# Attention and expert feed-forward on one core: the second split moved into the next feed-forward, attention shifted by 16 units, a ring of 13, division by the softmax sums in token rows, one dense projection

## What is computed

```python
# attention, 8 heads of 16 channels, over all 768 tokens of a batch
xf = layernorm(x)
q, k, v = xf @ Wq, xf @ Wk, xf @ Wv              # split into heads
att = q @ k.T / sqrt(16) + bias_time + bias_part # bias_part by pair of particles
att = where(causal in time, att, -inf)           # k's time step <= q's
x = x + (softmax(att) @ v).reshape(B, L, C) @ Wo

# feed-forward: 8 experts' weights, both top-2 gate values applied to all of them
p1, p2 = normalised top-2 of softmax(layernorm(x) @ Wg)
for p in (p1, p2):
    h = gelu((layernorm(x) * p) @ W1[e] + b1[e]) # for every expert e, width 512
    out += sum over e of h @ W2[e] + b2_sum
x = x + out
```

## Time and profile before

| | before |
| --- | --- |
| median of 3 runs | 2374.73 us (2370.79 to 2376.21) |
| the profiled execution's own time | 2375.36 us |
| its span, first to last instruction | 2373.6 us |
| PE busy | 93% |
| PEld busy | 85% |
| ACT busy | 68% |
| DVE busy | 55% |
| POOL busy | 45% |
| mean granted clock of TensorE | 0.969 |

### The profile page before, as it was taken

One profiled execution on the slowest core, in us unless ns is written; L12 is line 12 of the kernel. 1 busy time (PEld: TensorE's weight loads), 2 busy tenths in 40 slices (PEclk: granted clock), 3 DMA queues, 4 the chain that ended last, 5 costly groups with the idle time before them and its releaser, 6 DMA issues.

```text
span 2373.6 us, 48113 instructions
## 1 busy us (share of the span) xinstructions
PE 2212.2 (93%) x18213; PEld 2028.0 (85%) x18213; DVE 1309.2 (55%) x3191; ACT 1615.2 (68%) x2730; POOL 1063.1 (45%) x1051
## 2 busy tenths in 40 slices
PE   3779999999999999999998999999999999999998
PEld 2569898898988889898997988889898898988898
DVE  6246454755546466454755546466454755546453
ACT  2447677576776757677576776857677576776876
POOL 5124344443445344344443444344344443444366
PEclk7789999999999999999999999999999999999999
DMA  3412030220402212030220402212030220402200
GB/s 47 92 31 38 8 46 13 36 30 11 51 9 32 30 29 38 8 48 12 36 30 11 52 11 30 30 29 37 8 48 12 36 30 11 52 11 30 30 5 8
DMA packets 68528, 68.68 MB, mean 29 GB/s; under 512 B 20286, under 2 KB 53962, under 8 KB 68298
## 3 DMA queue, kind: packets, MB, share of 16 engines
q1 hardware_dynamic: 67634, 65.34, 19.4%
q10 hardware_dynamic: 664, 0.27, 0.0%
HBM read 10.83 MB, written 6.29 MB: 7 GB/s over the span
## 4 chain that ended last, share of the span: by engine, by line
PE 67%; DVE 17%; ACT 9%; issue 5%; POOL 1%; SPq 1%; DMA 0%; ACTq 0%; DVEq 0%; POOLq 0%
PE acc L925 20%; DVE maxes L682 7%; PE zps L914 6%; PE wide L857 6%; ACT z L535 6%; PE zps L916 6%; PE zps L915 6%; PE wide L845 5%; PE wide L828 4%; DVE h L745 3%; PE wide L871 2%; PE wide L879 2%; PE wide L864 2%; PE acc L902 2%; PE wide L811 1%
## 5 line engine op out<-in xcount | busy, mean ns | idle before, releaser
L469 POOL TENSOR_TENSOR h<-h 128x384 f32<-128x384 f32 x1024 | 1022.3, 1008 | 1236.3 <-ACT h L561 1225.6
L560 ACT ACTIVATE h<-zps,b_col 128x384 f32<-128x384 f32 x1024 | 591.6, 578 | 405.6 <-DVE h L745 346.7
L745 DVE TENSOR_TENSOR h<-zps,ratio_b 128x384 f32<-128x384 f32 x1024 | 542.3, 552 | 539.7 <-PE zps L916 528.5
L925 PE MATMUL acc<-w,h 128*128 128x128 f32 x6144 | 821.2, 277 | 0.2 <-DVE outt L754 0.2
L925 PEld LDWEIGHTS acc<-w,h 128*128 128x128 f32 x6144 | 800.5, 193 | 3.8 <-issue 0.5
L561 ACT ACTIVATE h<-h,b_col 128x384 f32<-128x384 f32 x1024 | 621.4, 607 | 0.0
L682 DVE TENSOR_REDUCE maxes<-wide 128x1 f32<-128x128 f32 (+5 forms) x768 | 430.2, 615 | 295.1 <-PE wide L828 293.6
L914 PE MATMUL zps<-x_hi,w_lo 128*128 128x384 f32 x1024 | 388.6, 379 | 11.5 <-ACT h L560 10.2
L535 ACT ACTIVATE z<-wide 128x896 f32<-128x896 f32 (+2 forms) x384 | 335.1, 916 | 33.9 <-PE wide L845 25.9
L915 PE MATMUL zps<-x_lo,w_hi 128*128 128x384 f32 x1024 | 347.9, 340 | 0.0
L916 PE MATMUL zps<-x_hi,w_hi 128*128 128x384 f32 x1024 | 347.1, 339 | 0.0
(11 more groups left out here) (99 smaller groups left out, 1469.3 us busy)
## 6 DMA issues: line engine op xcount, KB each, us to landing
stack<-halves SPq DMA_DIRECT2D x384, 96.0 KB, 3.1
stack<-halves SPq DMA_DIRECT2D x384, 24.0 KB, 2.6
out_dram<-outt SPq DMA_DIRECT2D x256, 24.0 KB, 1.6
x_in<-in_x SPq DMA_DIRECT2D x124, 48.0 KB, 2.4
stack<-max_rows SPq DMA_DIRECT2D x128, 3.0 KB
stack<-max_rows SPq DMA_DIRECT2D x128, 1.5 KB
w<-in_L_ffn_W SPq DMA_DIRECT2D x8, 256.0 KB, 4.0
stack<-z SPq DMA_DIRECT2D x2, 180.0 KB
```

The costliest lines, as they stand in the source:

```text
L469: pool.tensor_tensor(h1[:, PLACE[m], :], h0[:, m % 2, :], h1[:, PLACE[m], :], ALU.add).then_inc(hsum_ready, 1)
L560: act.activation(h0[:, m % 2, :], zps[BANK[m]][:, 0:CT], ACT.Gelu, bias=b1_col[:, j:j + 1]).then_inc(h0_ready, 1)
L745: vec.tensor_tensor(h1[:, PLACE[m], :], zps[BANK[m]][:, 0:CT], ratio_b[:, c * CT:(c + 1) * CT], ALU.mult).then_inc(z1_ready, 1)
L925: ins = pe.matmul(acc[:, n * P:(n + 1) * P], h1[:, PLACE[k], n * P:(n + 1) * P], w2[:, j, :], start=(j == 0 and n == 0), stop=(j == UNITS_ ...
```

## The change

Split 1 of a batch moves from slot 60 of the feed-forward before to slot 15.5 of the batch's own feed-forward; its second half of `xn` gets a buffer of its own (`xn_last`). All other attention steps come earlier, in most cases by some 6 to 16 slots, so that the first ones of a batch lie up to 16.5 slots before the feed-forward of the batch before begins. The ring has 13 places. The three runs of filler matmuls are gone. `sums` and `divide` are replaced: `tokens` transposes the mixed values with their sums into token rows, VectorE divides there, and `back` transposes 2 x 3 tiles back; the projection is one matmul per tile with a dense Wo. The output is added into `res` instead of `outt`. Round 0 has its own order (`squeezed`, `FIRSTS_ALONE`), and so has the last (`FIRSTS_LAST`).

```diff
-LAG = 4
-RING = 10
-FIRSTS = (2, 2, 1, 0, 1, 3, 0, 1, 2, 1, 2, 0, 2, 0, 2, 1, 0, 1, 1, 2, 0, 0, 0, 0, 0, 0, 0, 2, 3, 3, 0, 0,
-          1, 2, 1, 2, 2, 1, 0, 1, 3, 1, 0, 0, 0, 0, 2, 2, 3, 0, 1, 3, 1, 0, 0, 1, 0, 1, 0, 0, 0, 2, 0, 2)
-AT = {("stats", 0): -6.5, ("seed", 0): -5.0, ("root", 0): -5.0, ("scale", 0): -3.5, ("turn", 0): 0, ("query", 0): 0.5,
-      ("key", 0): 1.0, ("value", 0): 2.0, ("rows", 0): 16.5, ("mix", 0): 28.0, ("sums", 0): 32.5, ("divide", 0): 34.0,
-      ("rows", 1): 40.0, ("mix", 1): 46.5, ("sums", 1): 48.0, ("divide", 1): 51.0, ("project", 0): 52.0, ("project", 1): 52.0,
-      ("stats", 1): 52.0, ("turn", 1): 54.5, ("seed", 1): 54.5, ("root", 1): 56.0, ("gate", 0): 57.0, ("weigh", 0): 60.0,
-      ("split", 0): 60.0, ("split", 1): 60.0}
+LAG = 5
+FIRST_LAG = 5
+KNOTS = ((-4.950000000000001, 3.0), (10.5, 10.5))
...
+RESIDUAL_AT = 15
+RING = 13
+FIRSTS = (2, 1, 1, 2, 2, 0, 1, 3, 1, 0, 2, 2, 0, 1, 2, 1, 0, 0, 0, 0, 0, 1, 2, 3, 1, 1, 1, 1, 1, 3, 1, 3,
+          0, 0, 0, 0, 0, 0, 2, 2, 3, 3, 1, 1, 0, 2, 0, 1, 1, 0, 0, 0, 0, 0, 0, 0, 0, 2, 0, 2, 1, 2, 1, 1)
+AT = {("stats", 0): -16.5, ("seed", 0): -12.5, ("root", 0): -10.0, ("scale", 0): -7.0, ("turn", 0): -6.5, ("query", 0): -4.0,
+      ("key", 0): -4.0, ("value", 0): -1.5, ("rows", 0): 13.5, ("split", 1): 15.5, ("mix", 0): 23.0, ("rows", 1): 31.0,
+      ("tokens", 0): 31.0, ("mix", 1): 38.5, ("tokens", 1): 40.0, ("back", 0): 41.0, ("back", 1): 41.0, ("project", 0): 41.5,
+      ("project", 1): 42.0, ("stats", 1): 43.0, ("turn", 1): 43.0, ("seed", 1): 43.5, ("root", 1): 45.0, ("gate", 0): 47.0,
+      ("weigh", 0): 54.0, ("split", 0): 54.5}
+MAXIMA_AT = ((1.0, 1.5, 2.5, 3.5, 4.0, 5.0, 7.0, 7.5, 7.5, 10.0, 11.0, 12.0),
+             (22.0, 22.0, 22.5, 23.0, 23.5, 23.5, 24.5, 26.5, 28.0, 29.0, 30.0, 30.5))
+SCORES_AT = ((17.0, 17.5, 18.5, 18.5, 19.0, 19.0, 19.0, 20.0, 20.0, 20.0, 20.5, 21.0),
+             (32.5, 34.5, 34.5, 35.0, 35.5, 35.5, 36.0, 37.0, 37.0, 37.0, 37.5, 38.0))
...
+            for m in range(FIRST_LAG):
                 unit(first, m)
...
-                    if r.b > 0 and a == 0:
-                        vec.wait_ge(out_ready, r.at(CHUNKS, 1 - CHUNKS + 1))
...
+                if r.b > 0:
+                    vec.wait_ge(out_stored, r.at(16 * TPT * CHUNKS, 16 * (TPT * (c + 1 - CHUNKS) + 1)))
...
-                    if hh == 0 and part == 0:
-                        idle(w[:, 0:P], 3)
...
-                    if hh == 0 and part == 1:
-                        idle(acc[:, CT:CT + P], 5, start=False)
...
+                elif step == "tokens":
                     pe.wait_ge(*taken(r, "mix", a))
                     for i in range(TILES):
-                        ins = pe.matmul(w[:, i * GH:(i + 1) * GH], mixed[:, i * P:(i + 1) * P], pick[:, :], start=True, stop=True)
+                        ins = pe.transpose(w[:, i * P:(i + 1) * P], mixed[:, i * P:(i + 1) * P], ident[:, :])
                     ins.then_inc(wide_filled[s], 1)
...
+                elif step == "back":
+                    pe.wait_ge(*taken(r, "tokens", 1))
+                    for n in range(HT):
+                        ins = pe.transpose(w[:, n * P:(n + 1) * P], share[:, a * HT + n, :], ident[:, :])
                     ins.then_inc(wide_filled[s], 1)
                 elif step == "project":
-                    pe.wait_ge(*taken(r, "divide", 1))
+                    pe.wait_ge(*taken(r, "back", a))
                     for n in range(HT):
                         i = a * HT + n
-                        for g in range(GROUPS):
-                            ins = pe.matmul(w[:, n * P:(n + 1) * P], mixed_n[g][:, i * P:(i + 1) * P], wo_pad[:, g, :],
-                                            start=(g == 0), stop=(g == GROUPS - 1))
+                        ins = pe.matmul(w[:, n * P:(n + 1) * P], act_t[:, i * P:(i + 1) * P], wo[:, :], start=True, stop=True)
                     ins.then_inc(wide_filled[s], 1)
...
                 elif step == "split":
-                    if a == 0:
-                        idle(w[:, 0:P], 8)
-                    pe.wait_ge(xn_ready, r.at(4, 3 + a))
+                    pe.wait_ge(weighed, Round(r.b - a).at(2, 1 + a))
```

More of the change, by code:

```diff
@@ L76, in attention_plan @@
     plan += [(AT["mix", g], "mix", g) for g in range(GROUPS)]
-    plan += [(AT[step, g], step, g) for g in range(GROUPS) for step in ("sums", "divide")]
+    plan += [(AT[step, n], step, n) for step in ("tokens", "back") for n in range(2)]
     plan += parts("maxima", 1, MAXIMA_AT[1]) + [(AT["rows", 1], "rows", 1)] + parts("scores", 1, SCORES_AT[1])
@@ L87 @@
 PLAN = attention_plan()
-WIDE_STEPS = ("turn", "query", "key", "value", "maxima", "rows", "scores", "mix", "sums", "divide", "project", "gate", "split")
+WIDE_STEPS = ("turn", "query", "key", "value", "maxima", "rows", "scores", "mix", "tokens", "back", "project", "gate", "split")
 WIDE = {(s, a): n for n, (s, a) in enumerate([(s, a) for _, s, a in PLAN if s in WIDE_STEPS])}
@@ L96 @@
 assert sum(FIRSTS) == UNITS
+assert sum(FIRSTS_ALONE) + FIRST_LAG == UNITS + LAG and sum(FIRSTS_LAST) + LAG == UNITS
 def places(count):
@@ L114, with squeezed @@
 BANK_BACK = back(BANK)
+def squeezed(slot):
+    x0, y0 = PLAN[0][0], 0.0
+    for x, y in KNOTS:
+        if slot < x:
+            return int(2 * (y0 + (slot - x0) * (y - y0) / (x - x0))) / 2
+        x0, y0 = x, y
+    return slot
 class Round:
@@ L262, in build, with rounds, run @@
         block = ctx.enter_context(nc.Block())
-        def rounds(eng, attention, unit, after, prepare=None):
+        def rounds(eng, attention, unit, after, prepare=None, skipped=None):
             first = Round(0)
+            def run(r, step, a):
+                due = r.b > 0 if (step, a) == ("split", 1) else r.b < BATCHES
+                if due:
+                    attention(r, step, a)
+                elif skipped and (step, a) in WIDE and WIDE[step, a] <= WIDE["split", 1]:
+                    skipped(r, step, a)
             for _, step, a in PLAN:
-                attention(first, step, a)
+                run(first, step, a)
                 if prepare:
                     prepare(first, step, a)
[L276 to L279, removed]
+            for m in range(FIRST_LAG):
                 unit(first, m)
@@ L284, in steps @@
                     for r, start in ((following, 0), (ahead, UNITS)):
[L285 to L289, removed]
+                        for slot, step, a in PLAN:
+                            at = squeezed(slot) if r.b == 1 else slot + start
+                            if lo <= at < hi and r.b <= BATCHES:
+                                run(r, step, a)
+                m, firsts = LAG, FIRSTS
+                if this.b == 0:
+                    m, firsts = FIRST_LAG, FIRSTS_ALONE
+                elif this.b + 1 == BATCHES:
+                    firsts = FIRSTS_LAST
                 for k in range(UNITS):
                     steps(k, k + 0.5)
-                    for _ in range(FIRSTS[k]):
+                    for _ in range(firsts[k]):
                         if m < UNITS:
                             unit(this, m)
-                        elif following:
+                        elif following.b < BATCHES:
                             unit(following, m - UNITS)
@@ L897, in attention, with skipped @@
                     ins.then_inc(wide_filled[s], 1)
-            def idle(to, count, start=True):
-                for _ in range(count):
-                    pe.matmul(to, ident[:, :], ident[:, :], start=start, stop=start, skip_group_check=not start)
+            def skipped(r, step, a):
+                s, free, _ = wide_at(r, step, a)
+                if free > 0:
+                    pe.wait_ge(wide_free[s], free)
+                pe.sem_inc(wide_filled[s], 1)
+                pe.sem_inc(wide_free[s], 1)
             def unit(r, m):
@@ L927, in after @@
                 ins.then_inc(hsum_used, 1)
[L929 removed]
+            rounds(pe, attention, unit, after, prepare=prepare, skipped=skipped)
 WEIGHT_DMAS = 4
[L933 to L934 removed]
+POOL_SMALL = 11
+POOL_SET = 14
 BIAS_LOADS = 6
```

114 lines of the change are left out of this document (58 added, 56 removed).

## The result

The changed kernel took 2216.93 us, the median of 4 runs (2216.19 to 2218.14); the kernel before took 2375.47 (2370.79 to 2377.47) beside it. The ratio is 0.9336 with a 95% interval of 0.9320 to 0.9352: 158.5 us less, where 146 were forecast. The profiled execution took 2216.19 us, with a span of 2214.4.

What follows compares the result with a forecast made beforehand. TensorE, busy 93% of the span, was taken as the bound. 15 periods of 9.8 us saved, plus 3 at the start, minus 4 at the end, made 146 us off 2375.4: 2228 us forecast, 8-in-10 range 2172 to 2280.

Steps and rivals of the forecast that it cites:

- The sum and its total: Whole run: 9.8 us saved per period over 15 periods, 3 at the start, minus 4 at the end, 146 us.
- Work off TensorE: Division in token rows and dense projection: removed sums, broadcast and half the projection, less added transposes, save 4.7 us per period.
- The split: Between gate and first transposes: fillers 1.8, wait 3.0 (3.60 to 0.6) and clock loss 2.4 go, 7.2 us per period.
- The 2.4 for the clock: Behind the split: TensorE's half-clock work after the 3.60 us idle ends, saving 2.4 us per period (bounds 0 and 2.4).
- C: Rival: the split's wait, near 3.6 us, only moves to the turn with the low clock; 2309 us, chance 0.08.
- What is late next: New TensorE waits on VectorE per period: about 1.5 us at the turn, 0.75 at group 1's row maxima.
- The score stages: ScalarE's exponentials set both stages: 12.2 and 13.0 us elapsed, 7.0 lost beside 7.1 before, 0.1 saved per period.
- Fillers: In the score stages: removing 3.7 us of fillers per period gives nothing, because they stood in time that ScalarE sets.
- A: Rival: no new waits at turn, rows or split, each score stage loses 1 us less; 2157 us, chance 0.12.
- D: Rival: slower, the clock stays at 1.2 GHz through each score stage and the mix; 2537 us, chance 0.03.
- B: Rival: the clock falls in or behind the filler-free score stages, costing 2.4 us each; 2300 us, chance 0.13.

## Why the prediction was right, point by point

**The sum and its total.** 9.8 per period were forecast, and 6 less at the last. Measured: 10.8 for a full period (142.3 - 131.5), so 13 of them give 140.3 for 127.4 forecast, and the fourteenth, which in the kernel before ends without a wait at its split, 7.9. From mark to mark all else agrees: start and first period 12.8 forecast (9.8 + 3) and 13.0 measured, the last period with the end 5.8 forecast (9.8 - 4) and 7.9 - 2.1 = 5.8 measured. That agreement is luck. Counted from the same work, as above, the start gave about 7.5 and the last part about 11.3. The smaller division and projection alone had reached the split of batch 1 13.6 us earlier in their trace, so the new order at the start gave some of that back. How much the start gains by itself no run settles.

**Work off TensorE: right.** 4.7 forecast, 4.3 per period in the run that had only this part. The rest of the change then gave 138.1 - 131.5 = 6.5 per period, for 5.05 forecast (7.2 + 0.1 - 1.5 - 0.75).

**The split: right in size, and a condition was missing.** A wait of 0.6 forecast, 0.46 to 0.56 found; the clock of a period 1.00, as forecast. The 2.4 for the clock also fit: granted 0.50 for 3.4 us behind nine splits of the kernel before and for 6.3 to 6.8 behind five, 4.5 on average, which at half clock costs at most 2.3. The two orders that each undo a half of it (root ahead of weigh; normalisation behind, but units close behind the split) cost 24 us and gave nothing, so both halves are needed, and so is the second split's new place (58 us), which had no price of its own. For C I had written that the wait would move to the turn, and that 6.6 us of sums and units speak against it. The place in danger was not the turn but the fourth unit behind the split, which needs a free bank, thus a Gelu, thus a product by VectorE. I had not laid out the banks there.

**What is late next: the places right, the sizes a little high.** Turn 1.5 forecast, 1.01 found; rows 0.75 forecast, 0.79 found. The whole run's idle of TensorE by line shows the same trade. First of before (its turn is L806, its rows L833), then of after (turn L847, rows L874):

```profile
L806 PE MATMUL wide<-ident,xn 128*128 128x128 f32 x96 | 14.5, 292 | 9.9 <-DVE xn L667 9.9
L833 PE MATMUL wide<-ident,maxes 128*24 128x128 f32 x32 | 8.7, 273 | 5.8 <-DVE maxes L682 5.8
L894 PE MATMUL wide<-ident,xn 128*128 128x128 f32 x96 | 36.8, 393 | 50.5 <-DVE xn L717 50.5
```

```profile
L847 PE MATMUL wide<-ident,xn 128*128 128x128 f32 x96 | 14.9, 296 | 29.2 <-DVE xn L705 29.2
L924 PE MATMUL wide<-ident,xn 128*128 128x128 f32 x48 | 12.3, 290 | 10.3 <-DVE xn L763 10.3
L874 PE MATMUL wide<-ident,maxes 128*24 128x128 f32 x32 | 8.9, 279 | 13.3 <-DVE maxes L720 13.3
L957 PE MATMUL acc<-w,h 128*128 128x128 f32 x6144 | 824.7, 275 | 11.5 <-DVE res L797 11.5
```

The split gave back 40.2 us of idle, the turn took 19.3 and the rows 7.5. One wait was not in the sum: 11.5 us at the sum behind the rows (0.74 per period). It is VectorE's addition of chunk 0's output (L797, from 1156.91 to 1157.47), which has to read `acc` before the first sum of chunk 1 may overwrite it. The run that moved a first half behind sum 31 showed that this wait isn't on the path, as ScalarE is behind at that point.

**The score stages: right.** Group 0: 12.1 elapsed for 12.2, so 12.1 - 8.8 = 3.3 lost for 3.4. Group 1: 11.7, and with the 0.74 ahead of it 12.4, for 13.0; lost 3.0 for 3.6. This is the term that was mis-sized most, by 0.6 per period. ScalarE's timeline in the kernel after through group 0's stage, and two of TensorE's score parts in it:

```profile
1116.99 1.28 ACT L569 ACT_TABLE_LOAD   x1
1118.29 10.76 ACT L569 ACTIVATE z<-wide 128x896 f32<-128x896 f32 x12
```

```profile
1119.26 1.37 PE L884 MATMUL wide<-stack 128*128 128x256 f32 x6 [0.24 <-ACT z L569]
1121.11 2.26 PE L884 MATMUL wide<-stack 128*128 128x256 f32 x10 [0.48 <-ACT z L569]
```

One table load, then twelve exponentials without a gap, while TensorE waits for the buffers that they free: ScalarE sets the end, as the prediction had it. Load and exponentials take 12.06 us in either group. The prediction called 12.3 the least length of a stage; the windows are shorter than that because the last two exponentials run behind the last score part.

**The mis-sized terms together:** turn 0.5, split 0.1, stages 0.1 and 0.6, together 1.3 too little per period, and the removed work 0.4 too much. That leaves 0.9 too little; the measured period gave 1.0 more than the 9.8 forecast.

**Fillers: right for this order, wrong as a general statement.** "They stood in time that ScalarE sets; their cover was a wait" is true of their time. I had not given them a benefit. In the old order they had one of about 14 us by the single removals, 12 by the joint one. Had the change kept the old order and only dropped them, my sum for it would have been wrong by that.

**The rivals.** A (the new waits don't exist) and D (slower) didn't come true: the waits are there, and the time fell. B didn't come true in the changed kernel, and did in group 1's stage of the old order without fillers. The Trainium skill, "TensorE: Matmul & The Clock Gate", section "A second HAM failure mode: psum-queue depth-cycling", says that short idles between groups of matmuls are enough to make the clock swing. With that rule the trace of the old order without score fillers agrees (0.50 in the score stage in 9 of 13 periods, 9.1 us in all), and that of the changed kernel does not (1.00 through both stages, with waits for the exponentials between the parts). I gave B 0.13 on two microseconds of the start; the removal of the fillers shows that this row was weak evidence. Group 1's stage had three sums in the old order and has five in the new. That this is what holds the clock is argued, not shown: no run changed the number of sums in a stage alone. The length of the longest idle doesn't explain it: in the version with one first half moved, TensorE waits 1.25 or 1.26 us ahead of the third score part of group 1 in 11 of 13 periods, and the clock stays at 1.00 in all.

**Not settled.** The ring of 13 was not tried apart: the order of the changed kernel runs up to 13 first halves ahead of the sums and needs all places, so what it brings by itself stays open. The earlier place of the attention steps, the residual at slot 15 and the new start and end were not tried apart either.

## What to carry to other kernels

Where a stage is bound by another engine, count what the bounding engine needs there and lay the order out from it: that gave stage lengths within 0.6 us, the wait ahead of the second one included. When a wait is taken away by moving work of a busy engine, follow everything queued behind the moved work, buffers included: the wait came back at a bank, nine microseconds later, and took the whole gain. A filler costs its time and may hold the clock: taken out of the old order the fillers cost 12 us, put back into the new one 19. And choose marks that lie behind the same work in both kernels before you compare stretches of two traces.

## What the runs showed of the chip

The clock fell behind shorter idles than the 3.60 us seen before. In the version with root ahead of weigh, TensorE stood for 2.14 us at 1216.27 and worked at 1.2 GHz for most of the four microseconds behind it; after 2.32 us at 950.52 it stayed at 2.4 GHz. In the old order without score fillers it fell behind an idle of 1.33 to 1.47 us ahead of a score part in eight periods and behind one of 0.85 in a ninth (1539.32), and it held behind 1.34 in another (2111.10). The version of the changed kernel with one first half moved held it behind 1.26. In the changed kernel itself idles of 0.5 to 1.0 us, and stages full of short waits, left it at 2.4 GHz in every period.
